# Splitting the inverse row sums beside the maxima and spreading them with a 0/1 product, in an attention and mixture kernel

## The reference, cut to what matters

```python
qg = q.reshape(B, N_KV_HEADS, g, T, hd)              # 4 key heads, 4 query heads on each, hd = 32
scores = jnp.einsum('bgnqd,bgkd->bgnqk', qg, k) * scale
scores = jnp.where(causal, scores, -1e30)
attn = jax.nn.softmax(scores, axis=-1)
out = jnp.einsum('bgnqk,bgkd->bgnqd', attn, v)
...
x = x + attention(layernorm(x)); x = x + mixture(layernorm(x))
```

## Time and profile before

| | |
|---|---|
| median of 3 runs | 806.81 us (805.35 to 808.48) |
| profiled execution, its own time | 806.48 us |
| its span | 804.8 us |
| TensorE busy | 777.0 us (97%) |
| VectorE busy | 647.3 us (80%) |
| ScalarE busy | 575.6 us (72%) |
| GpSimd busy | 535.4 us (67%) |
| mean granted TensorE clock | 0.995 of full speed |

### The profile page before, as it was taken

How to read it: one execution, slowest core, us unless ns; L and a number is a source line. 1 busy time by engine, 2 the same in 40 slices (tenths; PEclk the granted TensorE clock), 3 DMA queues, 4 the chain that set the end, 5 groups by cost and what they waited for, 6 DMA issues and landing times. The chain is left out here.

```text
span 804.8 us, 15604 instructions
## 1 busy us (share of the span) xinstructions
PE 777.0 (97%) x4336; PEld 621.9 (77%) x4336; DVE 647.3 (80%) x1639; ACT 575.6 (72%) x1409; POOL 535.4 (67%) x685
## 2 busy tenths in 40 slices
PE   7788899999999999999999999999999999999998
PEld 6665677877777877777778778787778887788886
DVE  6768987899888877889788787888788787688774
ACT  3878787788876867788778767787777775654552
POOL 4586599783797769775687859776565615662572
PEclk9999999999999999999999999999999999999999
DMA  8323243654555456454445445444545345454550
GB/s 293 123 68 98 75 142 127 199 155 148 172 178 177 126 173 233 154 164 166 160 163 177 152 153 191 169 155 152 182 162 177 117 133 185 157 180 134 206 202 34
DMA packets 57053, 127.04 MB, mean 158 GB/s; under 512 B 10920, under 2 KB 28040, under 8 KB 56968
## 3 DMA queue, kind: packets, MB, share of 16 engines
q1 hardware_dynamic: 56968, 126.04, 46.9%
HBM read 107.55 MB, written 4.46 MB: 139 GB/s over the span
## 5 line engine op out<-in xcount | busy, mean ns | idle before, releaser
L1673 PE MATMUL u<-w_h,t_h 128*128 128x512 f32 x640 | 257.7, 403 | 0.7 <-issue 0.4
L1673 PE MATMUL u<-w_l,t_h 128*128 128x512 f32 x640 | 250.5, 391 | 0.0
L1673 PE MATMUL u<-w_h,t_l 128*128 128x512 f32 x640 | 250.5, 391 | 0.0
L1301 DVE TENSOR_TENSOR w_l<-w_raw,w_h 128x512 fp32r<-128x512 f32 x288 | 241.4, 865 | 0.3 <-ACT w_h L961 0.3
L961 ACT ACTIVATE w_h<-w_raw 128x512 fp32r<-128x512 f32 x380 | 216.7, 621 | 8.2 <-DMA w_raw<-in_w_units 7.0
L915 POOL TENSOR_TENSOR w_l<-w_raw,w_h 128x512 fp32r<-128x512 f32 x96 | 139.0, 1448 | 97.0 <-ACT w_h L961 96.9
L996 ACT ACTIVATE scores<-scores,mx 128x384 f32<-128x384 f32 (+1 forms) x224 | 128.8, 575 | 70.3 <-DVE mx L1244 69.0
L923 POOL TENSOR_TENSOR macc<-macc,gb 128x256 f32<-128x256 f32 x112 | 107.1, 960 | 58.5 <-DVE gb L1408 57.9
L1673 PEld LDWEIGHTS u<-w_h,t_l 128*128 128x128 f32 x640 | 120.2, 188 | 26.9
L1244 DVE CUSTOM_DVE_ANT_0 scores<-s,mask_qk 128x384 f32<-128x384 f32 (+1 forms) x224 | 112.3, 503 | 34.7 <-PE s L1549 33.4
L1673 PEld LDWEIGHTS u<-w_h,t_h 128*128 128x128 f32 x640 | 120.6, 188 | 25.3 <-issue 2.6
(11 more groups left out here) (155 smaller groups left out, 1216.6 us busy)
## 6 DMA issues: line engine op xcount, KB each, us to landing
w_raw<-in_w_units SPq DMA_DIRECT2D x160, 512.0 KB, 4.1
w_raw<-in_w_out_t SPq DMA_DIRECT2D x16, 512.0 KB, 4.4
w_raw<-in_shared_w_down SPq DMA_DIRECT2D x16, 512.0 KB, 4.6
q_st<-turned_h SPq DMA_DIRECT2D x224, 32.0 KB, 2.8
out<-x SPq DMA_DIRECT2D x16, 256.0 KB, 2.2
q_st<-turned_l SPq DMA_DIRECT2D x112, 32.0 KB, 2.8
x<-in_x SPq DMA_DIRECT2D x3, 1024.0 KB, 9.1
k_st<-turned_h SPq DMA_DIRECT2D x48, 32.0 KB, 2.8
```

The costliest lines, as they stand in the source:

```text
L1301: e.tensor_tensor(w_l[:, i % WR, k, :], w_raw[:, i % WR, k, :], f32(w_h[:, i % WR, k, :]), ALU.subtract).then_inc(s_wl, 1)
L1673: last = e.matmul(u_bank[n % 2][:], t[:, k, cols], ww[:, i % WR, k, :], start=(k == 0 and m == 0), stop=(k == KC - 1 and m == 2))
```

## The change

From span 8 on (24 spans; batches 1 to 3) the inverse sums take the maxima's way:

- VectorE takes the reciprocal in the span's slot 0, behind the second row maximum and no longer at the slot's end, and splits it into a high and a low part (`inverse_split`, two more instructions of 8 columns), beside the maxima's in `mhl`, which now has 16 columns.
- TensorE turns all 16 columns in one go, one slot later than the maxima were turned (slot 1 of the span), and `maxima_out` copies 16 rows, and `rows` carries 2 x 4 of them to `q_st`, both also one slot later. SyncE's `rows` thus stands behind the loads that its program has for slot 1.
- The turn is now two fp32r products with the identity instead of two fp32 transposes (in all 28 spans that have maxima).
- The inverse turn is one fp32r product of 256 columns, `chooser` (128x128, 0 and 1) by `m_t` (128 x 256), at the head of slot 3 instead of slot 5; GpSimd's spreading copy is gone for these spans, and GpSimd makes `chooser` once in slot 52.
- `st2` shrinks to two buffers, `ident` becomes an fp32r tile, and GpSimd clears `m_t` at the start, ahead of the identity and the mask.

```diff
+INVERSE_ROWS, CHOOSER_SLOT, MAXIMA_LATER = 3, 52, 1
+    SPREAD = H * KV
-        mhl, m_t = sb("mhl", [P, 2, TH, 2 * G], F32R), sb("m_t", [2 * G, Q], F32R)
-        rrep, r_t = sb("rrep", [P, TH, P]), sb("r_t", [P, 2, Q])
+        mhl, m_t = sb("mhl", [P, 2, TH, 4 * G], F32R), sb("m_t", [P, Q], F32R)
+        chooser, r_t = sb("chooser", [P, TH, P], F32R), sb("r_t", [P, 2, Q])
...
-                if s == span_slot(u) + CORE[name]:
+                if s == span_slot(u) + CORE[name] + (MAXIMA_LATER if name == "maxima" and u >= SPREAD else 0):
...
+        def inverse_turn_in(s):
             for u in range(NU):
-                if s == span_slot(u) + core(u, name):
+                if s == span_slot(u) + (core(u, "inverse_turn") if u < SPREAD else INVERSE_ROWS):
                     return u
...
         def pool_engine(e):
             e.memset(half_neg[:], -0.5).then_inc(s_small, 1)
-            e.memset(ident[:], 0.0)
+            e.memset(f32(m_t[:]), 0.0)
+            e.memset(ident, 0.0)
...
+                if s == CHOOSER_SLOT:
+                    make_chooser()
-                if (u := of_span(s, "spread")) is not None:
+                if (u := of_spread_span(s, "spread")) is not None:
                     spread_inverse(u)
...
+                if u > SPREAD:
+                    e.wait_ge(s_rt1, u)
+                made = 2 * G if u < SPREAD else 4 * G
+                e.activation(m_t[0:made, :], short("maxima", u - KV)[0:made, 0:Q], ACT.Copy).then_inc(s_mout, 1)
...
+            def inverse_split(u):
+                r = u % 2
+                hi, lo = (mhl[:, r, :, i * G:(i + 1) * G] for i in range(2))
+                e.wait_ge(s_rinv, u + 1)
+                if u >= KV + 2:
+                    e.wait_ge(s_mt, u - KV - 1)
+                e.tensor_copy(hi, rinv[:, r]).then_inc(s_isplit, 1)
+                e.wait_ge(s_isplit, inverse_parts(u)[1] - 1)
+                e.tensor_tensor(lo, rinv[:, r], f32(hi), ALU.subtract).then_inc(s_isplit, 1)
...
                 for u, m in first_pass_tiles(s)[1:]:
                     row_max(u, m)
+                if (u := inverse_rows_in(s)) is not None:
+                    inverse(u)
+                    inverse_split(u)
...
             def maxima_turn(u):
                 e.wait_ge(s_mlo, u - KV + 1)
+                if u >= SPREAD:
+                    e.wait_ge(*inverse_parts(u))
+                first = 2 * G if u < SPREAD else 0
...
-                    last = e.transpose(bank[0:2 * G, t * P:(t + 1) * P], f32(mhl[:, u % 2, t, :]), ident[:])
+                    last = e.matmul(bank[0:4 * G - first, t * P:(t + 1) * P], mhl[:, u % 2, t, first:4 * G], ident_r[:],
+                                    start=True, stop=True)
...
             def inverse_turn(u):
+                if u >= SPREAD:
+                    e.wait_ge(s_rrep, SPREAD + 3)
+                    e.wait_ge(s_mout, u - KV + 1)
+                    e.wait_ge(*short_free("inverse", u))
+                    e.matmul(short("inverse", u)[:, 0:Q], chooser[:, 0, :], m_t[:],
+                             start=True, stop=True).then_inc(s_rt1, 1)
+                    return
```

More of the change, by code:

```diff
@@ L305, in maxima_in, with of_spread_span, inverse_parts, inverse_rows_in @@
             return u if u is not None and (u < H * KV) == first else None
-        def of_span(s, name):
+        def of_spread_span(s, name):
+            for u in range(SPREAD):
+                if s == span_slot(u) + core(u, name):
+                    return u
+            return None
+        def inverse_parts(u):
+            return s_isplit, 2 * (u - SPREAD + 1)
+        def inverse_rows_in(s):
+            for u in range(SPREAD, NU):
+                if s == span_slot(u):
+                    return u
+            return None
+        def inverse_turn_in(s):
             for u in range(NU):
-                if s == span_slot(u) + core(u, name):
+                if s == span_slot(u) + (core(u, "inverse_turn") if u < SPREAD else INVERSE_ROWS):
                     return u
@@ L711, in rows @@
                     e.wait_ge(*queries_read(u - QR))
+                first = 0 if u < SPREAD else 2 * G
                 for k in range(2):
                     e.dma_start(f32(q_st[MAXROW + k:MAXROW + k + 1, u % QR, :, :]),
-                                f32(m_t[k * G:(k + 1) * G, :])).then_inc(s_m[u % 2], 16)
+                                f32(m_t[first + k * G:first + (k + 1) * G, :])).then_inc(s_m[u % 2], 16)
             def store(g):
@@ L889, in spread_inverse, with make_chooser @@
                               ).then_inc(s_rrep, 1)
+            def make_chooser():
+                e.wait_ge(s_rt1, SPREAD)
+                rows = chooser[:, 0, :]
+                e.memset(f32(rows), 0.0).then_inc(s_rrep, 1)
+                by_head = lambda ap: ap.rearrange("p (j d) -> p j d", d=D)
+                e.wait_ge(s_rrep, SPREAD + 1)
+                e.affine_select(out=by_head(rows), in_=by_head(f32(rows)), compare_op=ALU.not_equal, fill=1.0, base=0,
+                                pattern=[[-1, G], [0, D]], channel_multiplier=1).then_inc(s_rrep, 1)
+                e.wait_ge(s_rrep, SPREAD + 2)
+                e.affine_select(out=by_head(rows), in_=by_head(f32(rows)), compare_op=ALU.not_equal, fill=1.0, base=-G,
+                                pattern=[[-1, G], [0, D]], channel_multiplier=1).then_inc(s_rrep, 1)
             def mask_probabilities(u, k):
@@ L987, in maxima_out @@
                     e.wait_ge(*max_rows(u - 1))
-                e.activation(m_t[:], short("maxima", u - KV)[0:2 * G, 0:Q], ACT.Copy).then_inc(s_mout, 1)
+                if u == KV:
+                    e.wait_ge(s_mask, 1)
+                if u > SPREAD:
+                    e.wait_ge(s_rt1, u)
+                made = 2 * G if u < SPREAD else 4 * G
+                e.activation(m_t[0:made, :], short("maxima", u - KV)[0:made, 0:Q], ACT.Copy).then_inc(s_mout, 1)
             def row_sum(u, m):
@@ L1478, in vector_engine @@
                     moments(g)
-                if (u := of_span(s, "inverse")) is not None:
+                if (u := of_spread_span(s, "inverse")) is not None:
                     inverse(u)
@@ L1520, in turn_stacked @@
                             copies = r3[:, n % 2, t * G + 2 * i + j].rearrange("p c d -> p (c d)")
-                            last = e.transpose(stack_banks(n)[i][0:MAXROW, j * Q + t * P:j * Q + (t + 1) * P], copies, ident[:])
+                            last = e.transpose(stack_banks(n)[i][0:MAXROW, j * Q + t * P:j * Q + (t + 1) * P], copies, ident)
                     last.then_inc(done, 1)
@@ L1559, in turn_probabilities @@
                         at = j * w + t * P - seen(u, k)
-                        last = e.transpose(pair[:, at:at + P], masked_scores(u, j * TH + t)[:, k * P:(k + 1) * P], ident[:])
+                        last = e.transpose(pair[:, at:at + P], masked_scores(u, j * TH + t)[:, k * P:(k + 1) * P], ident)
                 last.then_inc(s_pb, 1)
```

38 lines of the change are left out of this document (22 added, 16 removed).

## The result

The changed kernel takes 828.29 us (median of 6 runs, 825.72 to 832.49) against 806.0 (6 runs, 805.35 to 808.48): ratio 1.027, 95% interval 1.0253 to 1.0287. Forecast were 808.2, at most 816. The change makes the kernel slower by 22 us, more than any case of the prediction gave.

What follows compares the result with a forecast made beforehand. From batch 1 on TensorE bounds the kernel, by its instructions and the places where it waits. -2.6 - 1.4 + 5.0 + 0.4 = +1.4 us on 806.5 gives 807.9, as median 808.2 us; range 802.5 to 816.

Steps and rivals of the forecast that it cites:

- TensorE's instructions: Inverse turn as one 256-column product saves 2.6 us over 24 spans; maxima's turn as two narrow products saves 1.4 over 28.
- The rival of slow narrow products: In the maxima's turn, narrow fp32r products are slow: 5.6 us lost instead of 1.4 saved, 815.2 us; chance 0.32.
- The order of the shorts: Moved turns change TensorE's waits: slot 12's D1 stall goes, slot 13's comes; 5.0 us lost over three batches, 0.4 elsewhere.
- Here D1 waits for the second score tile: Slot 13: the second down turn waits for VectorE's read, so the filler follows 1.46 us later than before, in three batches.
- 1.46 x 3 = 4.4: Slot 13's delay over three batches, the lower bound of the 5.0 us loss, with VectorE's added 0.5 all given back.
- I count that as even: Turn of x: slot 9's old waits, 0.8 us in all, taken as balanced by new waits in slots 7 and 9.
- VectorE's instructions: Two added 8-column instructions, 0.5 us per span, 12 us on VectorE, costing time only in slots where VectorE is late.
- To it come the two added instructions: 0.5. I give back 0.3: 0.2 net: Slot 13: added instructions delay VectorE 0.5 us, GpSimd's missing copy returns 0.3; 0.2 net in each of three batches.
- VectorE on time in slot 13: Rival: VectorE catches up in slot 13, the 5.0 us loss goes and slot 12's 0.55 is gained, 801.5 us; chance 0.16.
- Maxima late: Rival: maxima land late and the second pass waits up to 1 us in half the spans, +6 to +12; chance 0.10.
- the 5.6 us: Time left from the maxima's turn to the second pass after the shift; 4.2 needed, so the shift was priced at nothing.
- Gains and losses cancelling: Rival: nothing measurable because inverse and maxima were hidden; called only the forecast's sum coming out near nil; no separate chance.

Runs made afterwards that it cites:

- e7_both_moves: Kernel before plus both moves (maxima's turn one slot later, inverse turn in slot 3 of the span), nothing else: 1.0113, +8.8 us.
- e10_moves_vector_work: Kernel before plus both moves, changed tile sizes, VectorE's early reciprocal and two splits nobody reads; old transposes and GpSimd's copy kept: 1.0314, +25.9 us.
- e17_moves_vector_clock: e10_moves_vector_work plus 25 transposes that nobody reads in slot 13 of each of batches 1 to 3: 827.42 us, 1.0249 to the kernel before.
- e14_moves_reciprocal: Kernel before plus both moves, changed tile sizes and VectorE's early reciprocal, without the two splits: 818.56 us, 1.0151.
- e9_vector_work: Kernel before plus changed tile sizes, VectorE's early reciprocal and two splits that nobody reads, no turn moved: 1.0077, +5.9 us.
- e1_maxima_later: Kernel before with only the maxima's turn, its copy and its DMAs one slot later from span 8 on: 1.0083, +6.5 us.
- e12_split_at_end: Changed kernel with the reciprocal and its splits as VectorE's last work of the slot: 1.0386 to the kernel before.
- e11_addresses_back: Changed kernel with `mx` and `sums` declared last, so `m_t` and what follows lie elsewhere: 1.0314 to the kernel before, 3 us slower than the changed kernel.

## Why the prediction was wrong

**The ledger.** In medians: order of the shorts +8.8, sizes +2.9, the two splits on top +14.2, narrow turn, chooser and no GpSimd copy -4.5 (832.78 to 828.29). Together +21.4, and the change measured +22.3. TensorE's waits account for most of it: from before to e7_both_moves the turns of x and down wait 7.1 us more (9.4 against 2.3), and from there to e10_moves_vector_work 6.7 more; with some 4 for the clock (the 5.4 less the 1.3 that the turn of x waits less in e17_moves_vector_clock, which the 6.7 has already) and 2.9 for the sizes this is about 21 of 25.9.

**TensorE's instructions: right.** Forecast -2.6 and -1.4, together -4.0; measured -4.5 as a remainder of two medians whose executions spread by 5 and 7 us, so good to some us, and -1.2 for the narrow turn alone. The narrow pair's 0.12 from start to start is below both the 0.13 and the 0.16 that the prediction considered, and 0.05 are lost behind it, as taken. The chooser product takes 0.12, and no 0.09 is lost behind it. The rival of slow narrow products (0.32) was wrong.

**The order of the shorts: places half right, size too small.** The new order by the rule of three was right, also that slot 12's stall goes and D1's comes in 13. "Here D1 waits for the second score tile" left out that D0 now stands third behind the *first* score tile, which before it did not. The sum for the pure move was still right: net of slot 12's gain I had 1.46 x 3 = 4.4, and in e7_both_moves the down turns wait 5.7 in all against 1.5 before, 4.2 more. What failed here is "I count that as even" for the turn of x: 3.7 in all (0.71 in slot 7 and 0.52 in slot 9, three times each) against 0.8 before, +2.9 with no work added.

**VectorE's instructions: the step that failed.** "To it come the two added instructions: 0.5. I give back 0.3: 0.2 net", in slot 13 only, so 0.6 us of the sum. Measured in its place: 14.2 us for the two splits (13.1 by the ratios, e14_moves_reciprocal to e10_moves_vector_work). From read to read 4.29 before becomes 5.38, 1.09 a batch in place of 0.2. The two sizes in the step were near: the splits take 0.46, and 0.44 is given back (4.29 to 3.85 in e14_moves_reciprocal; the pair, which the copy had overlapped, goes from 1.67 to 1.28), nearer to the whole 0.5 that the prediction had as its other case. Missing was a third term, 1.07 for the weight pair pushed onto GpSimd's. With the old order of the shorts that term is not there, and e9_vector_work has 4.51, 0.22 over before: the step was reckoned as if the moves left GpSimd's instants where they were, and moving the maxima's turn brings its split 0.6 nearer. Slot 9 had no price at all: 1.11, of it 0.86 until the pair starts and 0.25 in the pair. From these two places TensorE waits 7.3 us more (down turns 5.2 to 9.2, turn of x 1.6 to 4.9), and the clock falls behind the longer wait. GpSimd was looked at only as a source of relief, because a copy goes. The row that showed the danger, a split of up to 1.79 us, is in the earlier trace rows. In e10_moves_vector_work, which keeps the copy, the copy lies ahead of the pair and the 2.35 is the same.

**The clock: no term.** Behind slot 13's idle TensorE goes at the lower level for some products, which costs some 4 us over three batches. The prediction priced each wait at its length.

**The sizes: no term.** 2.9 us, open in cause.

**The rivals.** VectorE on time in slot 13: excluded by the D0 and D1 waits. Maxima late: the second pass never waits for the DMA out of `m_t` in the changed kernel or in e1_maxima_later, so the 5.6 us were enough. Gains and losses cancelling: they did not. None took VectorE's lateness further than the forecast itself did, so the range ended at 816.

**Still open.** Why filler products start further apart with other sizes and places of tiles; most of the 3.0 us that VectorE's work costs with the old order, where TensorE's idle time from 155 to 790 us grows by 1.2 only (3.3 to 4.5); the last 5 us of e10_moves_vector_work's 25.9; why moving the maxima's turn brings GpSimd's split 0.6 nearer, which is about what D1 no longer waits in slot 12 (0.55).

## What to carry to other kernels

Before you add even 0.3 us to an engine that another one waits for, look up which of its next instructions share a port with a third engine, and shift them by that amount against the third engine's instants: two instructions of 0.17 us cost 1.5 us in slot 13 and 1.1 in slot 9 here. If the same change also shifts the third engine, shift it in the reckoning too: neither shift alone made the two meet. After a change of the order of shared buffers, price each use against its new predecessor, all of them and not the one that stands out. And where waits of TensorE stand close together, add what the products behind them may lose at the lower clock; filling the gap with transposes that nobody reads gave back 5.4 us here, some 4 of it by the clock.

## What the runs showed of the hardware

- In slot 12 a pair of VectorE's 128x512 subtractions takes 1.28, 1.67 or 2.35 us, with GpSimd's subtraction of the same shape beginning 0.89 behind its start, with GpSimd's copy beside it, or with GpSimd's subtraction beginning 0.43 behind its start.
- An 8-column copy to fp32r takes 0.17 in slot 12, where GpSimd is idle, 0.40 in slot 9, where GpSimd has work at the same time, and 1.00 in e12_split_at_end, where it ends at 190.25, 0.02 behind GpSimd's subtraction.
- An fp32r pair of 128 columns goes in 0.12 us, the time of one product of 256 columns, and costs 0.05 behind it; an fp32 pair 0.14 and 0.09.
- Behind D0's and D1's idle (2.20 and 0.86 in batch 1) the granted clock was 0.50 in the changed kernel, and products went at 0.43 in all three batches. It is not sure to fall: in e10_moves_vector_work batch 1 kept full speed after 2.25 and 0.86, in e7_both_moves all batches after 1.13 and 0.86, and in e14_moves_reciprocal in batch 3 seven starts lay 0.41 to 0.43 apart after 0.97 and 0.86, and in batch 2 none after 0.96 and 0.86.
- Cutting one small tile in SBUF (`st2`), with the wait that goes with it, cost 1 to 3 us, with 192 fewer of the filler starts at 0.22 us. Declaring two tiles elsewhere (e11_addresses_back) took those at 0.24 us from 354 to 485. Why is open.
